# Cross-attention block and a second attention on one core: where the score tiles of the maxima stand in TensorE's order

## The reference

```python
q = (layer_norm(x) @ q_w + q_b)          # 16 heads of 16
k = ctx @ k_w + k_b
v = ctx @ v_w + v_b
attn = softmax(q @ k.T / sqrt(16))       # per batch and head, 256 x 512
hidden = (attn @ v) @ cproj_w + cproj_b + x
y = gelu(layer_norm(hidden) @ fc_w + fc_b) @ proj_w + proj_b
h = hidden + y
probs = softmax((h @ w_q.T) @ (ctx @ w_k.T).T / sqrt(256))
out = h + alpha * (probs @ (ctx @ w_v.T)) @ w_o.T
```

## Time and profile before

| | |
|---|---|
| median of three runs | 314.23 us |
| lowest and highest | 312.45 and 318.35 us |
| span of the profiled execution (first to last instruction) | 310.4 us |
| whole time of that execution | not listed by itself; the median lies 3.8 us above the span |
| TensorE busy | 268.6 us, 87% |
| VectorE busy | 206.8 us, 67% |
| ScalarE busy | 187.8 us, 61% |
| GpSimd busy | 118.3 us, 38% |

### The profile page before, as it was taken

How to read it: one execution, slowest core, us unless ns; L and a number is a source line. 1 busy time by engine, 2 the same in 40 slices (tenths; PEclk the granted TensorE clock), 3 DMA queues, 4 the chain that set the end, 5 groups by cost and what they waited for, 6 DMA issues and landing times.

```text
span 310.4 us, 5591 instructions
## 1 busy us (share of the span) xinstructions
PE 268.6 (87%) x2073; PEld 195.3 (63%) x2073; DVE 206.8 (67%) x367; ACT 187.8 (61%) x351; POOL 118.3 (38%) x174
## 2 busy tenths in 40 slices
PE   3974769998788999899979997999998989898995
PEld 2670236683266676665866766665966777677974
DVE  5774777729657859576569598657388655366854
ACT  1553367759464686967454887766466678426622
POOL 3574652523111369830012688430131256324100
PEclk9997599989797999999999999999999999999999
DMA  5597552522254002124112112121130000000001
GB/s 176 173 155 104 141 157 94 163 72 67 78 154 126 12 25 67 57 74 126 64 38 99 28 59 70 34 80 51 34 130 3 0 1 2 2 0 0 2 34 36
DMA packets 21163, 21.62 MB, mean 70 GB/s; under 512 B 4608, under 2 KB 17616, under 8 KB 21136
## 3 DMA queue, kind: packets, MB, share of 16 engines
q1 hardware_dynamic: 16880, 13.09, 14.8%
q0 software_dynamic: 1648, 3.87, 4.9%
q10 hardware_dynamic: 2608, 4.30, 4.6%
HBM read 10.50 MB, written 1.05 MB: 37 GB/s over the span
## 4 chain that ended last, share of the span: by engine, by line
PE 56%; ACT 13%; POOL 11%; DVE 9%; issue 5%; DMA 3%; ACTq 2%; POOLq 0%; DVEq 0%
PE work_ps L602 10%; PE om L679 8%; PE s L652 7%; PE work_ps L589 6%; PE s L669 6%; PE work_ps L606 5%; DVE neg_max L1442 4%; ACT q_stack L1100 3%; ACT probs L1109 2%; POOL y_l L1833 2%; PE s L602 2%; DMA q_stack<-qp 2%; POOL kf L1793 1%; ACT fx L1136 1%; POOL ft L1828 1%
## 5 line engine op out<-in xcount | busy, mean ns | idle before, releaser
L1442 DVE TENSOR_REDUCE neg_max<-s 128x1 f32<-128x512 f32 x128 | 83.5, 683 | 23.1 <-PE s L652 21.9
L1109 ACT ACTIVATE probs<-s 128x512 f32<-128x512 f32 x128 | 75.3, 601 | 32.4 <-PE s L669 31.8
L652 PE MATMUL s<-k_stack,q_stack 97*128 97x512 bf16 x128 | 49.8, 424 | 8.2 <-DMA q_stack<-qp 4.9
L669 PE MATMUL s<-q_stack,k_stack 109*128 109x256 bf16 x256 | 51.8, 286 | 2.0 <-ACT probs L1109 1.0
L679 PE MATMUL om<-probs,vals 128*17 128x256 f32 x512 | 34.5, 390 | 0.2 <-ACT probs L1109 0.2
L669 PEld LDWEIGHTS s<-q_stack,k_stack 109*128 109x128 bf16 x256 | 21.0, 102 | 19.0 <-ACT probs L1109 5.0
L652 PEld LDWEIGHTS s<-k_stack,q_stack 97*128 97x128 bf16 x128 | 13.0, 102 | 28.8 <-DVE neg_max L1442 14.3
L1763 POOL CAST max_cols<-neg_max 128x8 bf16<-128x8 f32 x16 | 6.1, 381 | 63.2 <-DVE neg_max L1442 63.2
L1100 ACT ACTIVATE q_stack<-om 13x1024 bf16<-13x1024 bf16 x16 | 16.3, 1017 | 9.1 <-PE om L659 8.8
L679 PEld LDWEIGHTS om<-probs,vals 128*17 128x17 f32 x512 | 12.0, 98 | 13.7 <-issue 6.2
L1123 ACT ACTIVATE y_h<-work_ps 128x512 fp32r<-128x512 f32 x12 | 7.2, 596 | 16.3 <-PE work_ps L606 14.5
(11 more groups left out here) (328 smaller groups left out, 724.5 us busy)
## 6 DMA issues: line engine op xcount, KB each, us to landing
k_stack<-kp SPq DMA_DIRECT2D x96, 64.0 KB
q_stack<-qp SPq DMA_DIRECT2D x81, 32.0 KB
cx<-in_ctx_dram SPq DMA_DIRECT2D x4, 512.0 KB, 4.7
pcx<-in_ctx_dram ACTq DMA_DIRECT2D x3, 512.0 KB, 3.6
xz<-in_x_dram SPq DMA_DIRECT2D x4, 256.0 KB, 2.7
raw_late<-in_L_xattn_fc_w_dram POOLq DMA_DIRECT2D x1, 1024.0 KB, 5.4
raw_late<-in_L_xattn_proj_w_dram POOLq DMA_DIRECT2D x1, 1024.0 KB, 6.7
h<-in_x_dram ACTq DMA_DIRECT2D x3, 256.0 KB, 2.6
```

Of the source, the lines that this page charges most:

```text
L652: pe.matmul(s1[:, s1_bank(b, SLOTS * g + s), :], q_stack[0:ROW_MAX, hd, chunk(t)], k_stack[0:ROW_MAX, hd, :], start=True, stop=True).then_ ...
L669: mm = pe.matmul(s2[:, s2_bank(b, SLOTS * g + s), i * LQ:(i + 1) * LQ], k_stack[:, hd, chunk(k)], q_stack[:, hd, :], start=True, stop=True)
L1109: act.activation(probs[:, g % 2, s // 2, k:k + 2, :], s2[:, s2_bank(b, SLOTS * g + s), :].rearrange("p (k n) -> p k n", k=2), ACT.Exp).the ...
L1442: dve.tensor_reduce(neg_max[:, g % 2, s % 2, s // 2:s // 2 + 1], s1[:, s1_bank(b, SLOTS * g + s), :], AX.X, ALU.max, negate=True).then_inc ...
```

## The change

The tuple goes. Score tiles are numbered through, n = 32 x batch + 8 x group + slot; the slot with number n issues tile n + 10, so one tile in every slot, as long as there is one. Since ten is one group and two slots, slots 0 to 5 of a group hold tiles 2 to 7 of the next, and slots 6 and 7 hold tiles 0 and 1 of the one after. The prologue makes tiles 0 and 1 of (0,1) behind `max_rows(0, 0)`, ahead of the two waits. VectorE's reductions follow the same order. `split_max` and `max_rows` stay in slots 5 and 6.

```diff
-MAX_TILES = ((0, 1), (2, 3), (4,), (5,), (6,), (7,), (), ())
+MAX_LEAD = 10
...
+        def max_at(b, g, s):
+            n = NS * b + SLOTS * g + s + MAX_LEAD
+            return [(n // NS, n % NS // SLOTS, n % SLOTS)] if n < NS * B else []
...
                 for s in range(SLOTS):
                     max_tile(0, 0, s)
                 max_rows(0, 0)
+                for s in range(MAX_LEAD - SLOTS):
+                    max_tile(0, 1, s)
                 pe.wait_ge(w_lo, 3)
...
                 if part == 0:
-                    nb, ng = ahead(b, g)
-                    if not (isinstance(nb, int) and nb == B):
-                        for i in MAX_TILES[s]:
-                            max_tile(nb, ng, i)
+                    for tile in max_at(b, g, s):
+                        max_tile(*tile)
...
                 prepare("WA")
+                for s in range(MAX_LEAD - SLOTS):
+                    take_max(0, 1, s)
...
             def attend(b, g, s):
-                nb, ng = ahead(b, g)
-                if not (isinstance(nb, int) and nb == B):
-                    for i in MAX_TILES[s]:
-                        take_max(nb, ng, i)
+                for tile in max_at(b, g, s):
+                    take_max(*tile)
```

## The result

The changed kernel took 316.97 us, median of four executions (315.47 to 318.12), beside 313.56 us for the kernel before (four executions, 312.45 to 318.35): a ratio of 1.0113, 95% interval 1.0063 to 1.0163. That is within the 2% which count as no change, but 3.6 us above the forecast of 313.4, and on the other side of no change. It also turned out to be a number that a few executions can't settle: the old order itself, run again as an experiment, came to 1.0103 against itself.

A forecast was written before the change was run, and what follows sets the result against it. The kernel was taken as close to TensorE-bound, busy 87% of 310.4 us. Terms -1.05 - 1.2 + 0.8 + 0.7 gave about -0.8 us, so 313.4 us from a median of 314.23; range 308 to 318.

The forecast's parts named there:

- Bank waits: Score tiles waiting for their bank after 40 us: of 2.6 us in 8 waits, four waits give 1.2 us.
- GpSimd's chain: Ahead of the `max_rows` waits near 128 and 193, GpSimd comes late; some 1.4 us saved before it gain 0.
- Tiles hidden in `max_rows` waits: At five of six late group ends, the next group's tile 0 in slot 6 fills the wait: 1.05 us gained.
- The tile of (0,2): Batch 0, slot 6: tile 0 waits for key transfers, landing 41.4, delaying statistics and `cT_l`: cost 0.8 us, bounds 0 and 2.5.
- the sum: All terms over the whole kernel: about -0.8 us, 313.4 us; give or take 2 us, chance 0.50.
- the clock's rival: TensorE's low-clock stretches: 311.8 us if slots 6 and 7 keep it up, 315.0 if a wait at 66.2 lowers it; 0.15.
- The tile of (1,0): Slot 22, reached at 66.2: tile 0 waits 1.4 us for keys landing at 67.6; cost 0.7 us, bounds 0 and 3.2.
- The transfers decide: Both key landings, for (0,2) and (1,0), late: costs 5.7 us against gains of 2.25, 317.7 us; chance 0.20.
- VectorE was the cause: Two maxima per slot make tile 7's maximum late; every `max_rows` and bank wait goes, 303.7 us; chance 0.15.

The follow-up runs named there:

- the repaired order: The new order for all groups but (0,2) and (1,0), which keep their old places: 310.05 us, ratio 0.9878; run a second time 312.01 us, ratio 0.9924.
- the change in full: The new order for all groups, against the kernel before: 316.97 us, ratio 1.0113; again from a table of slots 314.54 us, ratio 0.9977.
- all but (0,2): The new order, except that the tiles of group (0,2) stand in their old places: 311.44 us, ratio 0.9931 to the kernel before.
- the control: The old order written as a table, instruction for instruction the kernel before: 317.43 us, median of 6, ratio 1.0103.
- batch 0 alone: The new order for groups (0,1) to (1,0) only, the old one from (1,1) on: 320.38 us, ratio 1.0038 to the kernel before.
- the earlier keys: The new order for all groups, with mask row and keys of (0,2) issued from GpSimd's queue instead of SP's: 312.40 us, ratio 0.995.

## Why the prediction went wrong

**Bank waits (-1.2 us): right in kind, more than right in size.** They are gone. Their gain ahead of GpSimd's chain was waited away, as forecast, but in another place: not at the next `max_rows` but in slot 20, where the waits for `kf` rose from 0.5 to 3.1 us together. The others gave more than 1.2 us: from slot 25 of batch 2 to slot 1 of batch 3 alone 1.1, of which 0.5 is given back by slot 6.

**Tiles hidden in `max_rows` waits (-1.05 us): right in size, at two places of five.** The waits at 128.30 and 193.53 fell from 1.39 us to 1.18 and 1.17, the 0.21 us that a tile takes. In the first trace of the change the latter is

```profile
200.88 0.32 PE L664 MATMUL om<-ident_b,max_cols 128*109 128x128 bf16 x2 [1.17 <-POOL max_cols L1774]
```

The waits of 1.87 us at 79.15 and of 0.84 us at 238.41 didn't change at all, and the one at 42.20 gave way to the wait for keys. So some 0.4 us are seen, not 1.05. Both terms together were forecast at 2.25 us, some 1.8 of it behind batch 0; that part measures 2.3 us on the traces and 2.6 in the table.

**The tile of (0,2) (+0.8 us): the step that failed, in its size.** The landing was taken at 41.4; the tile starts at 40.8 and 40.7 in the two traces of the change and at 42.0 to 42.3 in three variants, so that half was fair, though by luck: the transfers were issued earlier than in the trace of before, and the last took 5.8 us and more where the forecast had 4.5. The other half was "Slot 6 begins near 40.6", from one execution. In these five traces the level rises between 37.7 and 38.8 and not at 40.1, and TensorE is there at 39.2 to 39.5, over a microsecond earlier, while the keys come when they come: waits of 1.4 us in the two traces, 2.5 and 3.1 in two variants. Beside the repaired order with the same rise the group's move cost 2.15 and 1.96 us at slot 11, where the sum had 0.8 and an upper bound of 2.5. The path was the forecast's, through the late statistics: 1.2 us were forecast for `cT_l`, the product behind it came 1.4 and 1.3 us late. The 0.42 us taken off for slots 0 and 1 is seen too, in slot 9. What the sum lacked is the 1.1 to 1.2 us added from there to slot 11, with TensorE longer at 1.2 GHz. The sum carried no clock for this wait; the clock's rival had one only for the wait at 66.2. Taking the wait away in two ways (the tile back in its old place, the keys earlier) brought 311.4 and 312.4 us against 314.5; by their ratios alone the three can't be told apart, at the upper clock they can (309.1 and 310.0 against 311.8). No trace of the change has the level rise at 40.1, so what the tile costs then is not shown.

The Trainium skill, "TensorE: Matmul & The Clock Gate" (What's actually happening), says that the gate's timing doesn't start with the kernel, so that the moment of the change of level varies from run to run. The traces agree: 40.1 us in the execution of before, 37.9 in that of the change, and 40.2 and 37.9 in the two traces of the repaired order, which are of one kernel.

**The tile of (1,0) (+0.7 us): under-sized in batch 0, with another mechanism.** The forecast was a wait for the landing. In the change in full there is none; with (0,2) spared it is 0.8 us. Yet by slot 27 the tiles' new place costs 1.7 to 2.4 us in every trace that has it, above the forecast. In three traces, that of all but (0,2) among them, about 1 us of it is back at slot 8 of batch 1, where a stretch at 1.2 GHz near 95 us is missing that the repaired orders have; but the control lacks it too, with the tiles in their old place, so that this is the tiles' doing isn't shown. Over whole executions the cost isn't seen: median spans of 309.1 us with the tiles in the new place (9 executions) and 309.4 without (17).

**The rivals.** "The transfers decide" named the right place and the right mechanism for (0,2), but not its price as a whole: 5.7 us were worked out for two late landings, and batch 0 alone costs 2.2 us at the upper clock. In its own traces the change in full is 4.3 and 4.5 us behind the repaired order at slot 27, about half of it from one late landing. The 2.0 us that the prediction quotes from the Trainium skill, "DMA: Bandwidth & Descriptors", stand there in the section on the anatomy of one DMA on GpSimd's path; for these transfers on SP's queue the traces have 5.8 us and more. "VectorE was the cause" is out: the split's waits are unchanged (63.5 and 63.2 us), and those at `max_rows` are still there. That the two tiles in slots 6 and 7 keep the clock up, the fast side of the clock's rival, was not seen.

**The sum.** -0.8 us was forecast, a ratio of 0.997. The four executions said +3.4, with three of the four in the lower class of the clock; twelve more, beside 29 of before, said none (0.9977, close to the forecast's own ratio, with an interval of 0.4% to each side); the table says +0.9 us at the upper clock. So where the sum came near, it was by luck: more lost in batch 0 than forecast, and a little more gained behind it. What stays open is whether the change also shifts how often the lower clock comes: 8 of 16 with it, 36 of 78 before, but 3 of 17 with the repaired order, 1 of 9 with all but (0,2) and 1 of 12 with the earlier keys. The last three point to a gain there that no trace here explains.

## What to carry to other kernels

Moving work earlier in an in-order queue moves its waits earlier too: check each moved instruction's operands against the earliest moment at which the queue can reach it in any execution, not against the one in the profile at hand. Then follow the late operand through every queue that it holds up: here the tile's own wait was soon taken back, and VectorE's work behind it was what came late. A reordering need not be good or bad as a whole; here one group of sixteen gave back much of what the others gained, and leaving that group alone made a kernel faster than the one before and, at a like clock, than the change. Where executions of one kernel differ by 2% with the clock, compare at a like clock, run a control of the old kernel before believing 1%, and keep in mind that a change can move the clock itself.

## What was not expected of the hardware

The mean granted clock of one unchanged kernel ranged from 0.934 to 0.967 over 78 executions on three chips, and with it the span from 310.3 to 317.6 us. And the key transfers of (0,2) were slower on SP's queue than the forecast allowed for. The six issues in the change in full and in batch 0 alone (ns min/median/max of one, first and last start):

```profile
L534 SPq DMA_DIRECT2D k_stack<-kp x6: 558/592/596, 31.9 to 35.0; - x6
```

```profile
L544 SPq DMA_DIRECT2D k_stack<-kp x6: 557/594/1228, 32.0 to 35.2; - x6
```

The waiting tile starts at 40.83 and 42.30, that is 5.8 and 7.1 us behind the last issue, where the earlier trace rows have 3.9 to 6.1 us on GpSimd's queue. Issued from GpSimd's queue from 30.4 on, the same transfers landed within 2.5 to 3.4 us; they also went at an earlier time, so that the queue is the reason isn't shown. One of the six issues can take much longer than the others (1.23 us here, 2.16 us in the trace of before), so the forecast's even division of the row was a little off as well: there the last issue started at 37.2, not 36.9.
